# A mixture-of-experts layer: second set of row buffers for the gathers, scatters issued as a block, indices taken one expert later

## The reference, cut to what is computed

```python
xn = _layernorm(x, axis=-1)                       # x: (2, 2048, 256)
s = _L0_attn_ref(xn, W_qk, W_v, alibi_slope)      # causal attention with a linear bias
g = _silu(_L0_ffn_ref(xn, Wr, W1, W2))            # E = 8 experts, F = 1024
return x + s * g
# _L0_ffn_ref: every token goes to its best expert, at most 512 tokens for each;
#   h = relu(xe @ W1[e]);  ye = (h @ W2[e]) * p_tok;  y[token] = ye
```

## Time and profile before

| | |
|---|---|
| median of three runs | 537.84 us (535.86 to 539.24) |
| profiled execution, its own time | 539.47 us |
| its span | 537.7 us |
| busy: PE, DVE, ACT, POOL | 83%, 66%, 47%, 41% of the span |
| granted TensorE clock over the span | 0.946 of full speed |
| chain that ended last, by line, inside the expert loop | `tops<-wmax` 5%, `wall<-tops` 4%, `pmax` L788 6%, `w_l` L804 4% of the span |

### The profile page before, as it was taken

One profiled execution on the slowest core, in us unless ns is written; L12 is line 12 of the kernel. 1 busy time (PEld: TensorE's weight loads), 2 busy tenths in 40 slices (PEclk: granted clock), 3 DMA queues, 4 the chain that ended last, 5 costly groups with the idle time before them and its releaser, 6 DMA issues.

```text
span 537.7 us, 8673 instructions
## 1 busy us (share of the span) xinstructions
PE 447.9 (83%) x3094; PEld 300.6 (56%) x3094; DVE 354.0 (66%) x937; ACT 255.0 (47%) x535; POOL 222.6 (41%) x338
## 2 busy tenths in 40 slices
PE   5419779889999898989999999988897888798940
PEld 2114446557677765667766786655454555465630
DVE  4525849877676667876856645977677676867430
ACT  1203335346454634544533466766656565658520
POOL 4013835440423181732040002267475747466752
PEclk9776979999999998999999999999999899899985
DMA  2967470360610295224005244185948585753131
GB/s 81 270 221 234 163 230 5 66 181 2 188 49 1 41 320 152 80 43 157 0 35 99 34 143 131 3 245 98 228 85 239 98 226 101 236 99 90 61 99 38
DMA packets 70683, 65.49 MB, mean 122 GB/s; under 512 B 42374, under 2 KB 64524, under 8 KB 68592
## 3 DMA queue, kind: packets, MB, share of 16 engines
q1 hardware_dynamic: 64480, 47.67, 33.4%
q0 software_dynamic: 5632, 16.73, 11.1%
q10 hardware_dynamic: 528, 0.52, 0.3%
HBM read 31.27 MB, written 25.44 MB: 105 GB/s over the span
## 4 chain that ended last, share of the span: by engine, by line
DVE 29%; PE 26%; DMA 18%; ACT 9%; POOL 8%; issue 6%; SPq 2%; POOLq 0%; ACTq 0%; DVEq 0%
PE bank L1031 8%; PE bank L1032 7%; PE bank L1033 7%; DVE pmax L788 6%; DMA tops<-wmax 5%; DVE w_l L804 4%; DMA wall<-tops 4%; ACT sc L942 4%; PE bank L1098 4%; DVE hid_l L822 3%; DVE sc L757 3%; DMA slots<-empty 3%; DVE pT_l L770 2%; DMA raw<-in_w_e 2%; DMA sc<-in_w_e 2%
## 5 line engine op out<-in xcount | busy, mean ns | idle before, releaser
L1031 PE MATMUL bank<-w_h,hid_h 128*128 128x256 f16 x256 | 70.3, 275 | 11.9 <-DVE w_l L804 7.4
L948 ACT ACTIVATE pT_h<-bank 128x512 f16<-128x512 f32 (+2 forms) x80 | 42.0, 528 | 73.4 <-PE bank L1098 73.1
L1031 PE MATMUL bank<-v_h,pT_h 128*128 128x256 f16 x272 | 74.2, 273 | 0.4 <-DVE pT_l L770 0.4
L1032 PE MATMUL bank<-v_l,pT_h 128*128 128x256 f16 x272 | 74.2, 273 | 0.0
L1033 PE MATMUL bank<-v_h,pT_l 128*128 128x256 f16 x272 | 74.2, 273 | 0.0
L942 ACT ACTIVATE sc<-sc,nbias 128x512 f32<-128x512 f32 (+2 forms) x80 | 51.8, 649 | 45.1 <-DVE nbias L763 45.1
L770 DVE TENSOR_TENSOR pT_l<-bank,pT_h 128x512 f16<-128x512 f32 (+2 forms) x80 | 48.5, 607 | 36.8 <-ACT pT_h L948 36.8
L822 DVE TENSOR_TENSOR hid_l<-hid,hid_h 128x512 f16<-128x512 f32 x64 | 46.9, 739 | 35.8 <-ACT hid_h L965 35.8
L1032 PE MATMUL bank<-w_l,hid_h 128*128 128x256 f16 x256 | 70.2, 274 | 0.0
L1033 PE MATMUL bank<-w_h,hid_l 128*128 128x256 f16 x256 | 70.1, 274 | 0.0
L561 POOL DMA_INDIRECT back<-rows,get_idx x32 | 35.0, 1095 | 83.3 <-issue 83.3
(11 more groups left out here) (143 smaller groups left out, 963.5 us busy)
## 6 DMA issues: line engine op xcount, KB each, us to landing
raw<-in_w_e SPq DMA_DIRECT2D x5, 2048.0 KB, 11.6
sc<-in_w_e SPq DMA_DIRECT2D x3, 2048.0 KB, 10.5
slots<-empty SPq DMA_DIRECT2D x1, 4224.0 KB, 14.5
out<-xg SPq DMA_DIRECT2D x8, 512.0 KB, 3.5
rows<-xg SPq DMA_DIRECT2D x8, 512.0 KB, 4.6
rows<-so SPq DMA_DIRECT2D x8, 512.0 KB, 3.4
xg<-in_x SPq DMA_DIRECT2D x7, 512.0 KB, 3.9
wall<-tops SPq DMA_DIRECT2D x8, 128.0 KB
```

The source lines that it names most:

```text
L948: a_.activation(pT_h[:, t % 2, c * GTOK:c * GTOK + w], tr_ps[n % 2][:, 0:w], ACT.Copy).then_inc(pT_hi, 1)
L1031: pe.matmul(ps, a_h, b_h, start=first, stop=False, skip_group_check=shared)
L1032: pe.matmul(ps, a_h, b_l, start=False, stop=False, skip_group_check=shared)
```

## The change

Three edits go together. There are two sets of four row buffers: the old ones, and a second set that is a view of the two `xg` buffers; the experts take them in turn. POOL's `expert(e)` no longer waits for its own scatters before the gathers of e + 1: it first asks that the scatters of e - 1 have landed, makes all four blocks, issues the four scatters one behind the other, waits for `idx_made` and issues the four gathers. And DVE's `take_rows` for expert e moves from step 6 of expert e - 1 to step 2 of expert e itself, behind `hidden` and ahead of the third `split_low` (the one of expert 0 stays where it was, ahead of the loop). The last expert's operations on DVE only name the other buffers.

```diff
-        back = [sb(f"back{j}", [P, 2 * D]) for j in range(SJ)]
+        back = [[sb(f"back{j}", [P, 2 * D]) for j in range(SJ)],
+                [xg[j // 2].rearrange("p g d -> p (g d)")[:, j % 2 * 2 * D:(j % 2 + 1) * 2 * D] for j in range(SJ)]]
...
-                    back[j][:, :], None, rows[:, :],
+                    back[k][j][:, :], None, rows[:, :],
...
-                    back[j][:, 0:D], None, bounds_check=T - 1, oob_is_err=False).then_inc(out_put[j], 16)
-
-            def expert(e, k):
-                for j in range(SJ):
-                    pool.wait_ge(gate_made, e * SJ + j + 1 + 2 * SJ)
-                    pool.wait_ge(back_in[j], e * 16 + 16)
-                    g_.tensor_tensor(gate[:, j, :], gate[:, j, :], back[j][:, D:2 * D], ALU.mult).then_inc(gated, 1)
-                    pool.wait_ge(gated, e * SJ + j + 1)
-                    g_.tensor_tensor(back[j][:, 0:D], gate[:, j, :], back[j][:, 0:D], ALU.add).then_inc(done_made, 1)
-                    put(e, k, j)
-
+                    back[k][j][:, 0:D], None, bounds_check=T - 1, oob_is_err=False).then_inc(out_put[j], 16)
+
+            def put_landed(e):
                 for j in range(SJ):
                     pool.wait_ge(out_put[j], e * 16 + 16)
                 pool.sem_inc(put_over, 1)
+
+            def expert(e, k):
+                if e:
+                    put_landed(e - 1)
+                for j in range(SJ):
+                    b = back[k][j]
+                    pool.wait_ge(gate_made, e * SJ + j + 1 + 2 * SJ)
+                    pool.wait_ge(back_in[j], e * 16 + 16)
+                    g_.tensor_tensor(gate[:, j, :], gate[:, j, :], b[:, D:2 * D], ALU.mult).then_inc(gated, 1)
+                    pool.wait_ge(gated, e * SJ + j + 1)
+                    g_.tensor_tensor(b[:, 0:D], gate[:, j, :], b[:, 0:D], ALU.add).then_inc(done_made, 1)
+                for j in range(SJ):
+                    put(e, k, j)
+
                 pool.wait_ge(idx_made, e + 2)
...
+                    if e and f == 2:
+                        take_rows(e)
                     if more:
...
-                        if f == NF - 2:
-                            take_rows(e + 1)
```

More of the change, by code:

```diff
@@ L897, in _ @@
                 dve.wait_ge(back_in[j], E * 16)
-                v.tensor_tensor(gate[:, j, :], gate[:, j, :], back[j][:, D:2 * D], ALU.mult).then_inc(gated, 1)
+                b = back[(E - 1) % 2][j]
+                v.tensor_tensor(gate[:, j, :], gate[:, j, :], b[:, D:2 * D], ALU.mult).then_inc(gated, 1)
                 dve.wait_ge(gated, (E - 1) * SJ + j + 1)
-                v.tensor_tensor(back[j][:, 0:D], gate[:, j, :], back[j][:, 0:D], ALU.add).then_inc(done_made, 1)
+                v.tensor_tensor(b[:, 0:D], gate[:, j, :], b[:, 0:D], ALU.add).then_inc(done_made, 1)
         @block.scalar
```

## The result

The changed kernel takes **520.52 us** (median of 4 runs, 520.09 to 522.36) against 538.06 us (535.86 to 539.24) for the kernel before on the same chip: ratio 0.9685, interval 0.9646 to 0.9724, so 17.5 us less in the medians. The forecast was 525.5 with a range of 517.5 to 535. The profiled execution took 520.45 us and its span is 518.7 us, 19.0 less than before.

A forecast was written before the change was run, and what follows sets the result against it. Bound: a loop through SP and DVE (maxima, `tops`, weights, DVE's pieces), with gathers delaying `tops`. Terms -10 + 2.5 + 0.3 - 1.3 - 4.0 = -12.5 us gave 527.0 profiled, 525.3 from the median; written 525.5, range 517.5 to 535.

The forecast's parts named there:

- landings of `tops`, six: Expert loop: `tops` writes land late because of gathers under way; clearing them gives -11.3 us if all clear, -10 taken.
- end, POOL's first multiply of expert 6 to the last scatter: After POOL's last sums: gathers of expert 7 and each step behind them come earlier, -4.0 us, at most 4.5.
- weights: Five rounds' weight loads: about two more scatters fall into each load, 0.5 us a round, +2.5 us (0 to +6).
- DVE beside POOL: Last round: DVE's `w_l` pieces and `hidden` no longer run beside POOL's arithmetic, -1.3 us; elsewhere the load covers it.
- indices: `take_rows` moved to step 2: three small DVE operations, hidden in rounds with weights, bare in the last, +0.3 us.
- under a microsecond: Expert loop: margin between the last gather's landing at 23.3 us behind `wmax` and the next `tops`, at a period about 24.
- The two branches: Expert loop behind `tops`: `wall` with scales and first three pieces reaches the maxima less than 2 us before the weights.
- rival 3: Gathers delay `xeT`, PE waits ahead of an expert's first `up`: +12.5 us, so 550; chance 0.05.
- the cover that was named: DVE idles 2.15 us ahead of `wall`, so `xeT` up to 2 us late costs nothing, beyond it one for one.
- Number 1: Gathers are early but the loop doesn't feel it; weights lose what `tops` gains: -3, so 534.8 us; chance 0.17.
- number 2: All five `tops` at 2.81, weights no slower, PE's cover enough, `wall` landing sooner: -19.6, so 518.2 us; chance 0.13.
- number 4: The change doesn't do it: late indices hold POOL's gathers until 20 us or more, all stays at 537; chance 0.03.

## Why the prediction was right, and what was off

Forecast and result against the span of the profiled execution, since the terms were worked out on a trace:

| term | forecast | measured |
|---|---|---|
| landings of `tops`, six | -10 | -9.3 |
| end, POOL's first multiply of expert 6 to the last scatter | -4.0 | -4.6 |
| weights | +2.5 | -1.8 |
| the rest: DVE beside POOL, indices, start | -1.0 | -3.3 |
| sum | -12.5 | -19.0 |

The sum holds more than the medians do, since the profiled execution before lay 1.4 us above its median. And the rows are not independent: only two of the five loads, and five of the six `tops`, lie on the chain after the change, so the last row is a remainder and no measured cost. By the marks it is 0.5 us ahead of the loop, 1.0 in it and 1.8 between the last `tops` and POOL's first multiply of expert 6, a stretch that went from 25.7 to 22.9 us (1.0 of it `tops`) and is PE's in the changed kernel.

*`tops`.* Right in size and, by the run with the wait put back and the one without gathers, in cause. Five went from 24.09 to 15.76, the sixth from 4.07 to 3.08. The gathers stand where they were worked out, 14.7 us behind the first mark of the round (343.71 to 358.39; forecast 15), and the last at 18.7 (forecast 19.5). The margin ahead of the next `tops` was larger than the "under a microsecond" of the forecast, which had asked that the last gather be landed: the gathers' packets are over about 1 us and more ahead of `tops`, and with the scatters interleaved even an issue 2.7 us ahead cost nothing. Two things were finer than forecast. The second `tops` stays at 3.92 us, and that isn't the gathers' doing: without any gather it takes 3.87 (what else meets it in that round was not looked into, so of the 5.25 us before only some 1.3 were theirs). And in the run with held gathers, with the first gather always behind `tops`, it took anything from 2.60 to 4.48 us.

*The end.* First multiply to last scatter was 27.76 us (499.18 to 526.94) and is 23.17 (484.75 to 507.92), 4.6 less; forecast 4.0, with a cap of 4.5.

*The weights: the step that failed.* "Five rounds load weights: +2.5 us (0 to +6)" was the term that was mis-sized. The five loads went from 57.3 us (11.2, 11.4, 12.1, 10.5, 12.1) to 55.5 (10.9, 11.9, 11.4, 10.9, 10.4): no loss at all. All four scatters do lie in the load, as worked out, but the count of what is new was wrong: by POOL's timeline three of the four went out within each load before (in the example at 402.69, 406.15 and 410.36 us), so one was added and not "about two". And adding scatters costs the load nothing that can be told: the five loads sum to 56.9 us with the scatters interleaved, 56.9 without POOL's arithmetic and 56.3 without any gather, single loads lying between 10.4 and 11.9 us. So the right term was 0; the 1.8 us less are within what the loads differ by, and no cause is shown for them. What pays is the last scatter, 6.4 to 8.8 us in the run with the block alone. I asked what the added scatters do to the load and not what they find there.

*DVE beside POOL: right in kind, too narrow in place.* The forecast booked it in the last round only (-1.3), saying that in the others the load of the weights covers it. The two branches were nearly tied, as the prediction itself had read, and the chain before already went through `wall` and the pieces of `w_l` in three of the five rounds with weights. Two of them:

```profile
427.58 4.59 DMA wall<-tops
...
452.05 6.17 DMA wall<-tops
```

After the change it is three of five again; there each shorter piece counts. The loop lost 11.1 us, of which `tops` is 8.3: 2.8 are left, with the weights' 1.8 and the pieces overlapping in them, because a round is bound by the later of the two. The run with the scatters interleaved prices the block as 3.1 us of loop and 3.5 of end, of one execution each. So a term that is covered by one branch of a tie has to be counted as soon as the other term takes that branch away.

The Trainium skill ("SBUF — State Buffer", section "SBUF: two separate sides") calls the shared port of DVE and POOL an exclusive lock. The pieces' 972 ns beside spread arithmetic, 747 to 786 packed, and 745 to 747 with none fit that. The prediction had used the same rule against packing, since by it the splits of step 6 would stay at 2.6 us. They did not: in four of six rounds these two pieces take 1.41 us after the change, because POOL waits for the `Silu` and starts 1.6 us behind `tops` (393.63 against 392.00), when they are all but through, and no longer at about 0.9 us behind `wmax` as worked out.

*What was hidden, as forecast.* `take_rows` costs nothing (1.0018 alone). The later `xeT` does make PE wait, the sign that the prediction gave for rival 3: three times ahead of the first `up` of an expert, 2.8 us in all, where it was once and 0.2 us before. It is paid from the cover that was named: DVE still has idleness left ahead of `wall` in the first four rounds, 1.4 to 1.6 us (1.3 to 2.3 in the same rounds before, for one of them), though none in the last two:

```profile
387.82 0.38 PE L1039 MATMUL bank<-xeT,w_h 128*128 128x512 f16 x1 [1.26 <-issue]
```

```profile
401.06 0.42 DVE L803 TENSOR_REDUCE wtop<-wall 128x2 f32<-128x256 f32 x1 [1.59 <-DMA wall<-tops]
```

*The rivals.* Number 1, a loss given back by the weights, did not come, though the wait put back shows in small how a loop gives back a part (7.7 us more of `tops`, 5.3 of loop). The result of 520.52 us lies between my forecast and number 2 (518.2). In its parts it is nearer to number 2: the weights no slower, the end's cap reached. But the `tops` were not all at 2.81, and its half microsecond a round from an earlier `wall` is not there: in the three rounds of the chain `wall` took 5.8 to 6.1 us, no less than before (5.8, 4.6 and 6.2). So the time came near 518.2 partly by luck, through the terms of the last row. Number 3 shows only its wait of PE, number 4 did not occur.

## What to carry to other kernels

A small write that a loop waits for is priced by the transfers whose packets run beside it: look at its landing in each round, and move the bulk transfers that somebody can take early, until their packets are over when it is issued. Edits that only make room (a second buffer, a block of issues, earlier indices) can be worth nothing one by one, as the indices were here, so cost them as a set, and ask of each new order who waits for what it makes late. When you count what a new order adds to a transfer, count first what lies in it already. Where two branches of a loop are within a few microseconds of each other, a saving on the shared part and one on either branch don't hide each other for long: count both. And before a slower variant is put down to one wait, compare the granted clock of the two.

## What the runs showed of the hardware

A write of 1 KB from SBUF to DRAM with its completion took 2.6 to 3.2 us where no gather was on its way (3.3 to 3.9 in the second round of four kernels, with no gathers at all too; why is open). With gathers ahead of it, it depended on the last of the four: 4.1 to 7.1 us when that was issued between 1.0 us ahead of it and 1.7 us behind it, and, those second rounds aside, 2.6 to 3.1 us when it was issued 2.1 us or more ahead (3.0 at 2.1 us, in the run with only `take_rows` moved; 2.60 and 2.82 at 2.7 us). Its own packets, over at 1.03 us when alone, then lasted until 2.2 to 6.3 us in the kernel before. With the first gather 0.8 us behind it, it took 2.60, 2.84, 3.59, 4.48 and 4.48 us. So being beside the gathers' packets has the price, and an issue behind is no sure cure.

Scatters of 128 rows of 1 KB, issued as a block of four into a load of 2 MB, landed 7.3 to 10.2 us behind their issue for the first of the block and 6.4 to 8.8 us for the last; outside a load they took about 2.5 us. The load itself did not become longer (10.4 to 11.9 us with four scatters, 10.5 to 12.1 with three).

The same load of 2 MB took 10.9 us behind the spreading read of 128 KB (`wall`) and 7.7 us in the kernels without it. The packets show where the 3 us go: in the changed kernel those of `wall` run until 3.5 to 5.4 us behind the load's issue, and the first packet of the weights starts at 2.9 to 4.2 us, against 1.0 us in the kernels without `wall`. These kernels also issue the scatters elsewhere, but in the first of them all four go out 4.5 to 9.1 us behind the issue, much as in the changed kernel, and the last packet of the load still ends at 7.1 to 8.3 us, against 9.7 to 11.2. So the scatters are not the cause, and the read ahead is the likely one; no run changed it alone.
